# Other slots for the side jobs of a fused layer norm, attention and feed-forward kernel

## The chip, the cores and the metric

The kernel runs on one core of a Trainium2 chip. A core has TensorE (PE, the matrix engine), VectorE (DVE), ScalarE (ACT), GpSimd (POOL) and SyncE (SP), which here only issues DMAs. Each runs its own instruction list in order and waits on semaphores. The metric is the device time of one execution in microseconds (us), lower is better. Three runs of the kernel before gave 820.67, 822.58 and 823.44 us; the median is 822.58.

## The reference

For an input x of 16 batches, 512 tokens and 256 features:

```
xn  = layernorm(x)                              # no gain or offset
q, k, v = split(xn @ w_qkv.T + b_qkv)           # 16 heads of width 16
att = q @ k.T / 4 + bias[head, i - j]           # the bias hangs on the distance i - j
att = softmax(where(i >= j, att, -inf))         # causal
a   = (att @ v) @ w_proj.T + b_proj
f   = fp8(bf16(xn) / s_in) @ fp8(kernel / s_k) * s_in * s_k + ffn_bias
out = x + a + f
```

The position bias is folded into the score product as more rows of q and k, so one product of 64 rows a head gives scores and bias. Products in full precision are made of three products of a high and a low part.

## The kernel before

**Units and slots.** A batch is four units (g = 0 to 3) of four heads. A unit has 12 slots (k = 0 to 11). In each slot TensorE makes one block of transposed scores for the unit at hand (scores_T, line 611) into one of three PSUM banks scoreT_a to scoreT_c, and one block of plain scores two units ahead (scores, line 592) into one of three banks score_a to score_c. Slots 0 to 3 are blocks 512 wide, 4 to 7 are 384 wide, 8 to 11 are two tiles, 256 and 128 wide (of transposed scores; the plain ones likewise). In units 0 and 1 the transposed scores take a second product per tile, from the tile low_features (line 630).

**Who empties the banks.** ScalarE turns each transposed block into probs with an exponential (line 897). VectorE takes the row maximum of each plain block (line 975, two instructions a tile). The maxima of a unit are transposed by TensorE (job MT), negated and copied by ScalarE (max_T, line 819) and sent by SyncE (line 326) into the rows that the transposed scores of the next unit read. With three banks, slot n waits for the exponential of slot n - 3 (line 621) and for the maximum of slot n - 3 (line 600).

**Side jobs.** Between two slots TensorE does one side job, by a table of (unit, slot) pairs at the top of the file: PV (probabilities times v for the unit before, line 649, with the MT job inside it after its first tile), QK (four jobs a batch, each a q or k part of the next batch, line 537), V (two), FF (the fp8 product, two, line 580), PJ (output projection, two), T (two transposes of the normalised x of the batch after next, line 545). I call the slots between two jobs a spell. The jobs write the two banks misc_a and misc_b in turn, in the order in which they come (ORDER, MISC_BANK), and each waits until the job before it in its bank has been read out (misc, line 524).

**Read-outs.** ScalarE and VectorE read the job banks at places of the same kind of table, between exponentials and maxima: out_T (line 873) after PV, at slot OUT_AT; QK_evac (line 807, a copy of twice the width) and then QK_lo on VectorE (line 963); V_evac (line 792); FF (line 923); XH_evac and XB_evac (lines 796 and 799) and then T_lo on VectorE (line 957) for T. Since an engine's list is in order, an exponential that stands behind a read-out waits until that job is done. GpSimd masks the probs per third of a unit (line 1173) and does wide elementwise work between (lines 1161 to 1212).

**The loop.** Each engine's list is four bodies: batch 0, a loop over batches 1 to 13, batch 14, and batch 15.

Of the kernel before, what the change touches and what calls it, by code (L numbers as in the profile page):

```python
# [48 lines left out]

PV_AT = [(1, 3), (2, 3), (3, 3), (0, 3)]
MT_AT, FIRST_MT_AT = [(0, 3), (1, 3), (2, 3), (3, 3)], (0, 5)
QK_AT = [(0, 6), (0, 9), (1, 6), (1, 9)]
V_AT = [(2, 6), (2, 9)]
FF_AT = [(2, 0), (2, 0)]
PJ_AT = [(3, 0), (3, 6)]
T_AT, FIRST_T_AT = (3, 9), (0, 1)


OUT_AT = 4
FIRST_MT_OUT_AT = (0, 6)

MAX_AT, FIRST_MAX_AT = 2, (0, 4)
QK_HI_AT, QK_LO_AT = [(0, 6), (0, 9), (1, 6), (1, 9)], [(0, 7), (0, 10), (1, 7), (1, 10)]
V_OUT_AT = [(2, 6), (2, 9)]
AH_AT = [(2, 2), (2, 3)]
FF_OUT_AT = [(2, 0), (2, 1)]
RESULT_AT = [(3, 1), (3, 6)]
NORM_AT = [(3, 1), (3, 3), (3, 4), (3, 6)]  # L70
XH_AT, FIRST_XH_AT = [(3, 9), (3, 10)], [(0, 2), (0, 2)]
XL_AT, FIRST_XL_AT = [(3, 10), (0, 0)], [(0, 3), (0, 3)]

INVERT_AT, LAST_INVERT_AT = (0, 8), (3, 8)
STATS_AT, AGGR_AT = [(1, 2), (1, 3), (1, 5), (1, 8)], (1, 9)
MAGIC_AT = [(2, 0), (2, 1), (2, 2)]


EARLY = 4
# [6 lines left out]
ORDER = [(KINDS[kind], i) for _, kind, i in sorted((at, kind, i) for kind, ats in enumerate(  # L86
    (PV_AT, MT_AT, QK_AT, V_AT, FF_AT, PJ_AT, [T_AT, T_AT])) for i, at in enumerate(ats))]
assert len(ORDER) % 2 == 0
# [37 lines left out]
def build(nc, x, w_qkv, b_qkv, w_proj, b_proj, pos, ffn_w, s_in, s_k, ffn_b, feat_q, feat_k, out):  # L126
    with ExitStack() as ctx:
# [386 lines left out]
        def _(pe):  # L514
# [96 lines left out]
            def scores_T(b, g, k, first):  # L611


                n = SLOTS * g + k
                rows, u = rows_of(HU * g + k % 4)
                if k == 0:
                    if isinstance(b, int) and b == 0 and g < 2:
                        pe.wait_ge(feat_loaded[g], 64)
                    pe.wait_ge(max_loaded[g], 64 * (b + 1))
                if n >= 3 or not first:  # L620
                    pe.wait_ge(exp_done, ROW * b + n - 2)
                tiles = [k // 4] if k < 8 else [2, 3]
# [93 lines left out]
            def body(b, first, last, more):  # L716
# [62 lines left out]
        def _(act):  # L779
# [101 lines left out]
            def body(b, first, last, more):  # L881
                for g in range(G):
                    for k in range(SLOTS):
                        pb, pg = (b, g - 1) if g else (b - 1, 3)
                        if (g, k) == FIRST_MAX_AT if first and g == 0 else k == MAX_AT:
                            if not (last and g == 3):
                                max_hi(*((b, g + 1) if g < 3 else (b + 1, 0)))
                        if k == OUT_AT and not (first and g == 0):
                            if not (last and g == 3):
# [10 lines left out]
                        if not last:  # L900
# [38 lines left out]
        def _(dve):  # L939
# [133 lines left out]
            def body(b, first, last, more):  # L1073
                for g in range(G):
                    nb, ng = (b, g + 2) if g < 2 else (b + 1, g - 2)
                    ahead = not (last and g >= 2)
                    for k in range(SLOTS):
# [54 lines left out]
        def _(pool):  # L1132
# [55 lines left out]
            def add_bias(b):  # L1188
                pool.wait_ge(xn_ready, TT * (b + 1))
                pool.wait_ge(bp_made, 1)  # L1190
                xs = x_slot(b)
                GP.tensor_tensor(xs, xs, BP[:, :].unsqueeze(1).broadcast_to([P, TT, C]), ALU.add) \
                    .then_inc(xp_ready, 1)
# [83 lines left out]
            def body(b, first, last, more):  # L1277
                for g in range(G):
                    if g == 0:
                        quant_round(b)  # L1280
                    if g == 1 and not last:
                        quant_scale(b + 1)
                    if g == 2 and more:
                        rstd(b + 2)
                    if g == 3:
                        add_bias(b)
                    mask(b, g, 0)
                    if g == 0:
                        quant_write(b)
                        v_beside_ones(b, first)  # L1290
                    if g == 2 and not first:
                        attn_parts(b - 1)
                    if g == 3:
                        add_ffn(b)
                    mask(b, g, 1)
                    if g == 2:
                        ffn_bias(b)
                    if g == 1 and not first:
                        divide(b - 1)
                    mask(b, g, 2)  # L1300
# [35 lines left out]
```

## Time and profile before

| | |
|---|---|
| median of three runs | 822.58 us |
| the profiled execution | 822.72 us |
| its span | 821.0 us |
| busy share of the span | PE 92%, DVE 76%, ACT 71%, POOL 64% |
| TensorE clock in the steady part | full |
| one steady batch | 46.65 us (336.94 to 383.59) |

The span is what the profiler saw between first and last instruction; the execution is 1.7 us longer. The setup takes about the first 56 us, then 16 batches follow. In the timelines a row gives the start from the span's begin and the duration. Matmuls overlap, and their ends are modelled, so the time a job takes is read as the distance from its first start to the first start of what follows it.

### The profile page before, as it was taken

How to read it: one execution, taken by the hardware profiler on the slowest of the kernel's cores; microseconds unless marked ns; L12 is line 12 of the kernel's file. 1: busy time of each engine (PE TensorE's matmuls, PEld its weight loads, DVE VectorE, ACT ScalarE, POOL GpSimd, SP SyncE). 2: the span in 40 equal slices, each digit the busy share in tenths (PEclk: the TensorE clock that was granted, in tenths of full speed). 3: DMA queues.
4: the chain of work that ended last, by engine and by line, in shares of the span. 5: the costliest groups of instructions: out<-in, count | busy, mean ns of one | idle time of the engine just before them, and what ended most of it. 6: DMA issues, size and time to landing. Idle time of an engine off the chain costs nothing.

```text
span 821.0 us, 23167 instructions
## 1 busy us (share of the span) xinstructions
PE 756.7 (92%) x6313; PEld 521.4 (64%) x6313; DVE 627.6 (76%) x2395; ACT 585.5 (71%) x1258; POOL 529.1 (64%) x525
## 2 busy tenths in 40 slices
PE   6879999999999999999999999999999999999983
PEld 4556666676666767676666667666676667666552
DVE  3767878887878888887887888787887888787602
ACT  4246767777777868877786878877786787776650
POOL 6434568677676768677576867677676867757460
PEclk9759999999999999999999999999999999999885
DMA  5845666567765676667666666676567656766202
GB/s 170 158 77 100 113 154 115 138 132 140 152 134 139 122 163 116 135 148 142 133 134 151 117 149 124 133 159 136 134 134 157 116 135 137 144 132 130 65 17 84
DMA packets 55548, 106.07 MB, mean 129 GB/s; under 512 B 10464, under 2 KB 30432, under 8 KB 55520
## 3 DMA queue, kind: packets, MB, share of 16 engines
q1 hardware_dynamic: 55048, 105.19, 61.0%
q10 hardware_dynamic: 472, 0.54, 0.2%
q8 instruction: 13, 0.21, 0.1%
q14 instruction: 15, 0.12, 0.0%
HBM read 18.68 MB, written 8.91 MB: 34 GB/s over the span
## 4 chain that ended last, share of the span: by engine, by line
PE 58%; ACT 9%; SPq 8%; issue 8%; DVE 8%; DMA 6%; DVEq 1%; ACTq 1%; POOL 0%; POOLq 0%
PE misc_a L649 12%; PE misc_a L537 10%; SPq L326 7%; PE misc_b L537 7%; PE scoreT_b L627 6%; PE scoreT_a L627 5%; PE score_c L604 4%; PE misc_b L649 3%; PE score_a L604 3%; ACT probs L897 3%; ACT qk_parts L807 2%; DVE row_max L975 2%; DMA stacks<-neg_max_T 2%; ACT xnT_hi L796 2%; PE misc_b L588 2%
## 5 line engine op out<-in xcount | busy, mean ns | idle before, releaser
L1173 POOL TENSOR_SCALAR_AFFINE_SELECT probs<-probs 128x512 f32<-128x512 f32 x256 | 160.7, 640 | 243.4 <-ACT probs L897 241.6
L975 DVE CUSTOM_DVE_ANT_0 score_b<-score_b,causal_mask_q 128x384 f32<-128x384 f32 (+3 forms) x321 | 161.9, 521 | 122.1 <-PE score_b L604 121.8
L975 DVE CUSTOM_DVE_ANT_0 score_a<-score_a,causal_mask_q 128x512 f32<-128x512 f32 x319 | 173.2, 559 | 7.7 <-PE score_a L604 3.5
L975 DVE CUSTOM_DVE_ANT_0 score_c<-score_c,causal_mask_q 128x256 f32<-128x256 f32 (+3 forms) x384 | 171.4, 473 | 1.8 <-PE score_a L604 1.7
L897 ACT ACTIVATE probs<-scoreT_a 128x512 f32<-128x512 f32 (+1 forms) x256 | 145.0, 566 | 9.3 <-PE scoreT_a L630 6.4
L897 ACT ACTIVATE probs<-scoreT_b 128x384 f32<-128x384 f32 (+1 forms) x256 | 133.8, 523 | 24.4 <-PE scoreT_b L627 18.7
L975 DVE DVE_READ_ACCUMULATOR2_ANT row_max<- 128x1 f32 x1024 | 142.9, 140 | 0.0
L897 ACT ACTIVATE probs<-scoreT_c 128x384 f32<-128x384 f32 (+1 forms) x256 | 135.7, 530 | 8.2 <-PE scoreT_c L630 7.5
L649 PE MATMUL misc_a<-probs,v_ones 128*32 128x128 f32 (+3 forms) x1536 | 132.9, 442 | 0.4 <-POOL probs L1173 0.4
L627 PE MATMUL scoreT_a<-stacks 64*128 64x512 f32 (+3 forms) x320 | 109.5, 362 | 14.3 <-DMA low_features<-neg_max_T 7.5
L627 PE MATMUL scoreT_b<-stacks 64*128 64x384 f32 (+3 forms) x320 | 119.8, 394 | 2.3 <-ACT probs L897 2.0
L604 PE MATMUL score_b<-stacks 64*128 64x384 f32 (+3 forms) x321 | 118.8, 402 | 0.3 <-DVE row_max L975 0.2
L604 PE MATMUL score_a<-stacks 64*128 64x512 f32 x319 | 110.9, 379 | 3.2 <-DVE row_max L975 2.4
L627 PE MATMUL scoreT_c<-stacks 64*128 64x256 f32 (+3 forms) x384 | 105.4, 307 | 9.0 <-ACT probs L897 9.0
L604 PE MATMUL score_c<-stacks 64*128 64x256 f32 (+3 forms) x384 | 100.1, 314 | 7.2 <-DVE row_max L975 7.0
L627 PEld LDWEIGHTS scoreT_b<-stacks 64*128 64x128 f32 x320 | 57.0, 185 | 58.6 <-issue 27.8
L627 PEld LDWEIGHTS scoreT_c<-stacks 64*128 64x128 f32 x384 | 68.9, 187 | 16.0 <-ACT probs L897 14.1
L649 PEld LDWEIGHTS misc_a<-probs,v_ones 128*32 128x32 f32 x1536 | 59.9, 109 | 29.3 <-issue 12.9
L604 PEld LDWEIGHTS score_c<-stacks 64*128 64x128 f32 x384 | 66.8, 190 | 14.0 <-DVE row_max L975 13.9
L627 PEld LDWEIGHTS scoreT_a<-stacks 64*128 64x128 f32 x320 | 57.9, 188 | 24.8 <-issue 11.7
L604 PEld LDWEIGHTS score_a<-stacks 64*128 64x128 f32 x319 | 55.6, 189 | 17.9 <-DVE row_max L975 13.7
L873 ACT ACTIVATE out_T<-misc_a 128x512 f32<-128x512 f32 x48 | 28.7, 599 | 43.1 <-PE misc_a L649 42.7
(241 smaller groups left out, 1963.4 us busy)
## 6 DMA issues: line engine op xcount, KB each, us to landing
stacks<-qk_parts SPq DMA_DIRECT2D x128, 512.0 KB, 8.2
x_ring<-in_L_attn_x SPq DMA_DIRECT2D x16, 512.0 KB, 3.5
attn<-out_T SPq DMA_DIRECT2D x64, 128.0 KB, 2.6
xn<-recips SPq DMA_DIRECT2D x31, 256.0 KB
out<-x_ring SPq DMA_DIRECT2D x15, 512.0 KB, 3.0
stacks<-neg_max_T SPq DMA_DIRECT2D x128, 4.0 KB
low_features<-neg_max_T SPq DMA_DIRECT2D x124, 4.0 KB
low_features<-probs SPq DMA_DIRECT2D x8, 128.0 KB, 5.0
```

The source lines that it names most:

```text
L326: eng.dma_start(max_rows(g, h), MTS[2 * TT * h:2 * TT * h + 2 * TT, g % 2, :].bitcast(F32)) \
L537: last = mm(o, l(ct), r(ct), start=(ct == 0 and i == 0), stop=(ct == CT - 1 and i == 2))
L588: last = mm(bank[0:HU * 2 * TT, 0:P], MX[:, g % 2, 32 * part:32 * part + 32], ident[:, :], start=(part == 0), stop=(part == 1))
L604: last = mm(SB_[n % 3][:, o:o + w], STK[rows, u, 0, P * qt:P * qt + P], STK[rows, u, 1, 0:w], start=True, stop=True)
L627: last = mm(bank, STK[rows, u, 1, P * j:P * j + P], STK[rows, u, 0, P * j:T], start=True, stop=(g >= 2))
L649: last = mm(bank[32 * i:32 * i + 32, P * j:T], VA[:, j, HU * g + i, :, :].rearrange("p d a -> p (d a)"), probs(g, j)[:, i, :], start=(j == ...
L796: A(XH[:, ct, :], misc_of("T", ct)[:, :], ACT.Copy).then_inc(xh_ready, 1)
L807: A(qk_part(m, 0), misc_of("QK", m)[:, :].unsqueeze(1).broadcast_to([P, 2, T]), ACT.Identity, bias=BQ[:, bias:bias + 1]).then_inc(qh_ready, 1)
L873: A(OT[:, :], misc_of("PV", g)[:, :], ACT.Copy).then_inc(ot_ready, 1)
L897: A(probs_slot(g, k), STB[(SLOTS * g + k) % 3][:, 0:w], ACT.Exp).then_inc(exp_done, 1)
L975: last = V.tensor_tensor_reduce(bank, bank, CMQ[:, T - w:T], 1.0, LEAST, ALU.add, ALU.max, MX[:, g % 2, 8 * h + 4 + qt:8 * h + 5 + qt])
L1173: last = GP.affine_select(out=d, in_=d, compare_op=ALU.is_ge, fill=0.0, base=0, pattern=[[0, HU], [1, P]], channel_multiplier=-1)
```

## The change

The table of places is another one, and two GpSimd operations change places. The tables say (unit, slot):

```diff
-PV_AT = [(1, 3), (2, 3), (3, 3), (0, 3)]
+PV_AT = [(1, 2), (2, 2), (3, 2), (0, 2)]
-QK_AT = [(0, 6), (0, 9), (1, 6), (1, 9)]
-V_AT = [(2, 6), (2, 9)]
-FF_AT = [(2, 0), (2, 0)]
-PJ_AT = [(3, 0), (3, 6)]
-T_AT, FIRST_T_AT = (3, 9), (0, 1)
-OUT_AT = 4
+QK_AT = [(0, 6), (0, 10), (1, 6), (1, 10)]
+V_AT = [(2, 5), (2, 8)]
+FF_AT = [(2, 11), (2, 11)]
+PJ_AT = [(3, 5), (3, 8)]
+T_AT, FIRST_T_AT = (3, 10), (0, 1)
+OUT_AT = 3
...
@@ gpsimd body
                     if g == 3:
-                        add_bias(b)
+                        ffn_bias(b)
                     mask(b, g, 0)
...
                     if g == 2:
-                        ffn_bias(b)
+                        add_bias(b)
```

A job comes after its slot. The read-outs move with their jobs: QK_evac to (0, 6), (0, 10), (1, 6), (1, 10) and QK_lo one slot later; V_evac to (2, 5) and (2, 8); the FF read-outs to (2, 11) and (3, 0); the result sums to (3, 5) and (3, 8); XH_evac and XB_evac to (3, 10) and (3, 11); T_lo to (3, 11) and (0, 0). The inversion of the denominators moves from (0, 8) to (0, 7), the statistics of x from slots 2, 3, 5 and 8 of unit 1 to 2, 2, 3 and 3, their aggregation from slot 9 to 5, the three fp8 steps of VectorE from slots 0, 1 and 2 of unit 2 to 2, 2 and 3, and one normalisation from (3, 6) to (3, 7).

So the spells before are slots 4 to 6, 7 to 9 and 10 to 3 in unit 0, and now 3 to 6, 7 to 10, and 11 to 2. No amount of work changes.

First place: ScalarE in unit 1 of batch 0 (the loop has the same order), from the read-out of PV to the second read-out of QK. Before:

```order
L819 ACTIVATE neg_max_T<-misc_b 32x128
L873 ACTIVATE out_T<-misc_a 128x512
L897 ACTIVATE probs<-scoreT_b 128x384
L897 ACTIVATE probs<-scoreT_c 128x384
L897 ACTIVATE probs<-scoreT_a 128x384
L807 ACTIVATE qk_parts<-misc_a,b_qkv 128x2x512
L897 ACTIVATE probs<-scoreT_b 128x384
L897 ACTIVATE probs<-scoreT_c 128x384
L897 ACTIVATE probs<-scoreT_a 128x384
L807 ACTIVATE qk_parts<-misc_b,b_qkv 128x2x512
```

and now:

```order
L819 ACTIVATE neg_max_T<-misc_b 32x128
L873 ACTIVATE out_T<-misc_a 128x512
L897 ACTIVATE probs<-scoreT_a 128x512
L897 ACTIVATE probs<-scoreT_b 128x384
L897 ACTIVATE probs<-scoreT_c 128x384
L897 ACTIVATE probs<-scoreT_a 128x384
L807 ACTIVATE qk_parts<-misc_a,b_qkv 128x2x512
L897 ACTIVATE probs<-scoreT_b 128x384
L897 ACTIVATE probs<-scoreT_c 128x384
L897 ACTIVATE probs<-scoreT_a 128x384
L897 ACTIVATE probs<-scoreT_b 128x384
L807 ACTIVATE qk_parts<-misc_b,b_qkv 128x2x512
```

The read-out of PV (out_T) stood ahead of slot 4's exponential and now stands ahead of slot 3's; between two read-outs there are now four exponentials, not three.

Second place: TensorE in unit 3 of batch 0, around the T job (line 545). Before:

```order
L627 MATMUL scoreT_a<-stacks 128x256
L604 MATMUL score_a<-stacks 128x256
L627 MATMUL scoreT_a<-stacks 128x128
L604 MATMUL score_a<-stacks 128x128
L545 MATMUL misc_a<-ident_f,xn 128x128 x4
L545 MATMUL misc_b<-ident_f,xn 128x128 x4
L627 MATMUL scoreT_b<-stacks 128x256
L604 MATMUL score_b<-stacks 128x256
L627 MATMUL scoreT_b<-stacks 128x128
L604 MATMUL score_b<-stacks 128x128
L627 MATMUL scoreT_c<-stacks 128x256
L604 MATMUL score_c<-stacks 128x256
```

and now:

```order
L627 MATMUL scoreT_b<-stacks 128x256
L604 MATMUL score_b<-stacks 128x256
L627 MATMUL scoreT_b<-stacks 128x128
L604 MATMUL score_b<-stacks 128x128
L545 MATMUL misc_a<-ident_f,xn 128x128 x4
L545 MATMUL misc_b<-ident_f,xn 128x128 x4
L627 MATMUL scoreT_c<-stacks 128x256
L604 MATMUL score_c<-stacks 128x256
L627 MATMUL scoreT_c<-stacks 128x128
L604 MATMUL score_c<-stacks 128x128
```

The two transposes come one slot later, ahead of slot 11 alone.

Third place: VectorE in the loop, from the end of one batch to the start of the next; xnT_lo are the two T_lo, L975 the row maxima. Before:

```order
L957 TENSOR_TENSOR xnT_lo<-misc_a,xnT_hi 128x512
L332 REGISTER_ALU
L975 ISA score_c,row_max<-score_c,causal_mask_q 128x256
L975 ISA row_max 128x1
L975 ISA score_c,row_max<-score_c,causal_mask_q 128x128
L975 ISA row_max 128x1
L1108 REGISTER_ALU
L1108 COMPARE_AND_BRANCH
L975 ISA score_a,row_max<-score_a,causal_mask_q 128x512
L975 ISA row_max 128x1
L957 TENSOR_TENSOR xnT_lo<-misc_b,xnT_hi 128x512
```

and now:

```order
L975 ISA score_c,row_max<-score_c,causal_mask_q 128x256
L975 ISA row_max 128x1
L975 ISA score_c,row_max<-score_c,causal_mask_q 128x128
L975 ISA row_max 128x1
L956 ISA
L957 TENSOR_TENSOR xnT_lo<-misc_a,xnT_hi 128x512
L1108 REGISTER_ALU
L1108 COMPARE_AND_BRANCH
L975 ISA score_a,row_max<-score_a,causal_mask_q 128x512
L975 ISA row_max 128x1
L957 TENSOR_TENSOR xnT_lo<-misc_b,xnT_hi 128x512
```

T_lo of the first half stood ahead of slot 11's maxima and now stands behind them; that of the second half stays behind slot 0's.

## Rows read from the trace of the kernel before

**Rows 1.** Windows, one middle batch and the last: length, busy and count per engine, PEclk, DMA.

```profile
336.94:383.59 46.65, 44.68 (x396) 31.23 (x400) 38.47 (x149) 36.22 (x79) 32.46 (x32) 1.00 0.66 138
756.40:821.00 64.60, 45.68 (x347) 29.30 (x344) 20.89 (x75) 28.22 (x62) 26.08 (x24) 0.74 0.21 60
```

**Rows 2.** Timeline, TensorE, a middle batch's first unit: start, duration, line, operation.

```profile
383.52 1.06 PE L649 MATMUL misc_a<-probs,v_ones 128*32 128x512 f32 x8
...
386.23 0.44 PE L627 MATMUL scoreT_b<-stacks 64*128 64x384 f32 x1
...
386.51 0.33 PE L630 MATMUL scoreT_b<-low_features 64*128 64x384 f32 x1
...
387.03 0.34 PE L630 MATMUL scoreT_a<-low_features 64*128 64x384 f32 x1
...
387.30 0.50 PE L537 MATMUL misc_a<-xnT_hi,w_qkvT_hi 128*128 128x512 f32 x1
...
388.90 0.44 PE L627 MATMUL scoreT_b<-stacks 64*128 64x384 f32 x1
...
390.08 0.50 PE L537 MATMUL misc_b<-xnT_hi,w_qkvT_hi 128*128 128x512 f32 x1
...
391.68 0.38 PE L627 MATMUL scoreT_b<-stacks 64*128 64x256 f32 x1
...
394.66 0.50 PE L604 MATMUL score_c<-stacks 64*128 64x512 f32 x1 [0.45 <-DVE row_max L975]
...
395.74 1.07 PE L649 MATMUL misc_a<-probs,v_ones 128*32 128x512 f32 x8
```

**Rows 3.** Timeline, ScalarE, the same unit.

```profile
386.53 0.60 ACT L873 ACTIVATE out_T<-misc_a 128x512 f32<-128x512 f32 x1 [1.22 <-PE misc_a L649]
...
387.03 0.48 ACT L897 ACTIVATE probs<-scoreT_b 128x384 f32<-128x384 f32 x1
...
389.14 1.12 ACT L807 ACTIVATE qk_parts<-misc_a,b_qkv 128x1024 fp32r<-128x1024 f32 x1 [0.86 <-PE misc_a L537]
...
390.16 0.48 ACT L897 ACTIVATE probs<-scoreT_b 128x384 f32<-128x384 f32 x1
...
395.88 0.60 ACT L897 ACTIVATE probs<-scoreT_a 128x512 f32<-128x512 f32 x1
```

**Rows 4.** Timeline, TensorE, the other three units of that batch.

```profile
405.37 0.50 PE L627 MATMUL scoreT_a<-stacks 64*128 64x512 f32 x1 [0.56 <-DMA stacks<-neg_max_T]
...
405.99 0.61 PE L580 MATMUL misc_a<-ffn_w_q,xq 128*128 128x256 bf16 x4
...
406.96 0.50 PE L627 MATMUL scoreT_b<-stacks 64*128 64x512 f32 x1
...
407.93 1.06 PE L649 MATMUL misc_a<-probs,v_ones 128*32 128x512 f32 x8
...
416.63 0.39 PE L537 MATMUL misc_a<-w_projT_hi,attn_hi 128*128 128x256 f32 x1
...
418.26 0.49 PE L627 MATMUL scoreT_b<-stacks 64*128 64x512 f32 x1
...
419.15 1.07 PE L649 MATMUL misc_b<-probs,v_ones 128*32 128x512 f32 x8
...
425.42 0.66 PE L545 MATMUL misc_a<-ident_f,xn 128*128 128x128 f32 x4
...
426.44 0.38 PE L627 MATMUL scoreT_b<-stacks 64*128 64x256 f32 x1
...
430.30 1.06 PE L649 MATMUL misc_a<-probs,v_ones 128*32 128x512 f32 x8
```

**Rows 5.** Timeline, ScalarE, end of the batch's fourth unit.

```profile
426.24 0.62 ACT L796 ACTIVATE xnT_hi<-misc_a 128x512 fp32r<-128x512 f32 x1
...
427.19 0.54 ACT L897 ACTIVATE probs<-scoreT_b 128x384 f32<-128x384 f32 x1
```

**Rows 6.** Timeline, VectorE, start of the next batch.

```profile
429.66 0.68 DVE L957 TENSOR_TENSOR xnT_lo<-misc_b,xnT_hi 128x512 fp32r<-128x512 f32 x1
```

More of the change, by code:

```diff
@@ L47 @@
 QUERY_TILES = [(3,)] * 4 + [(2,)] * 4 + [(1, 0)] * 4
-PV_AT = [(1, 3), (2, 3), (3, 3), (0, 3)]
-MT_AT, FIRST_MT_AT = [(0, 3), (1, 3), (2, 3), (3, 3)], (0, 5)
-QK_AT = [(0, 6), (0, 9), (1, 6), (1, 9)]
-V_AT = [(2, 6), (2, 9)]
-FF_AT = [(2, 0), (2, 0)]
-PJ_AT = [(3, 0), (3, 6)]
-T_AT, FIRST_T_AT = (3, 9), (0, 1)
-OUT_AT = 4
+PV_AT = [(1, 2), (2, 2), (3, 2), (0, 2)]
+MT_AT, FIRST_MT_AT = [(0, 2), (1, 2), (2, 2), (3, 2)], (0, 5)
+QK_AT = [(0, 6), (0, 10), (1, 6), (1, 10)]
[4 more added lines that the diff above has]
+OUT_AT = 3
 FIRST_MT_OUT_AT = (0, 6)
 MAX_AT, FIRST_MAX_AT = 2, (0, 4)
-QK_HI_AT, QK_LO_AT = [(0, 6), (0, 9), (1, 6), (1, 9)], [(0, 7), (0, 10), (1, 7), (1, 10)]
-V_OUT_AT = [(2, 6), (2, 9)]
+QK_HI_AT, QK_LO_AT = [(0, 6), (0, 10), (1, 6), (1, 10)], [(0, 7), (0, 11), (1, 7), (1, 11)]
+V_OUT_AT = [(2, 5), (2, 8)]
 AH_AT = [(2, 2), (2, 3)]
[L68 to L76, printed above, removed]
+FF_OUT_AT = [(2, 11), (3, 0)]
+RESULT_AT = [(3, 5), (3, 8)]
+NORM_AT = [(3, 1), (3, 3), (3, 4), (3, 7)]
+XH_AT, FIRST_XH_AT = [(3, 10), (3, 11)], [(0, 2), (0, 2)]
+XL_AT, FIRST_XL_AT = [(3, 11), (0, 0)], [(0, 3), (0, 3)]
+INVERT_AT, LAST_INVERT_AT = (0, 7), (3, 8)
+STATS_AT, AGGR_AT = [(1, 2), (1, 2), (1, 3), (1, 3)], (1, 5)
+MAGIC_AT = [(2, 2), (2, 2), (2, 3)]
 EARLY = 4
```

## The prediction

> **What bounds the kernel now.** I read the windows first. In a steady batch of 46.65 us TensorE is busy 44.68, VectorE 38.47, ScalarE 36.22 and GpSimd 32.46 us, with TensorE's clock at 1.00, its upper level of 2.4 GHz [rows 1]. TensorE sets the time, but its busy figure hides short waits, so I went on to its timeline and measured each job and spell from first start to next start. I count a unit from its PV job to the next PV job.
>
> Unit 0 of a batch before [rows 2]: PV 2.71 (383.52 to 386.23), three slots 1.07, QK 1.60 (387.30 to 388.90), three slots 1.18, QK 1.60, six slots 4.06 (391.68 to 395.74), in all 12.22. The spells of three slots have no wait, since three banks take three slots. The spell of six has: the fourth block of its kind waited 0.45 for VectorE's maximum at 394.66. Unit 1 is 12.19 long with the FF job in it (395.74 to 407.93), unit 2 11.22 and unit 3 11.15 (to 430.30) [rows 2, 4]; the four are 46.78.
>
> The rule for what follows: the fourth slot of a spell can't start before the exponential of the spell's first slot is done. That exponential stands behind the read-out of the job just ended. So the price of a read-out at a spell's head is paid by TensorE as soon as the spell has four slots.
>
> **ScalarE's answer after a job** [rows 3]. After PV: out_T starts 3.01 after PV's start (386.53), the exponential behind it 0.50 later. After a QK job: the copy starts 1.84 after the job's start (389.14 after 387.30), the exponential 1.02 later (390.16) and takes 0.48, so it ends 3.34 after the job's start. A 512 wide exponential takes 0.60 (395.88). I add 0.05 for the semaphore, an estimate: in the row of 387.30 the job starts right behind the last product, so the gap is small, and ends of 0 and 0.1 move the sum by under 0.3 a batch.
>
> **What a slot costs when it had to wait.** Its two first products start together, the third 0.28 later (386.23, 386.51), and the job follows 0.27 after the last one (387.03, 387.30) [rows 2]: 0.55 for a 384 wide slot, and I take 0.58 for the two tiles of slot 10 (four starts instead of two, shorter each). A 512 wide slot with low_features I put at 0.65, by width from the same rows, and one without at 0.43, from 0.89 for three of them (418.26 to 419.15) [rows 4] plus what a restart loses (0.28 against 0.17 between 386.23, 386.51 and its followers).
>
> **Unit 0 after.** Slots 3 to 6: slot 3's exponential starts at 3.01 + 0.50 = 3.51, ends at 4.11, slot 6 starts at 4.16 and QK at 4.71. Without the wait TensorE would have been there at 2.71 + 1.07 + about 0.48 for slot 3 = 4.26. Slots 7 to 10: slot 10 starts 3.39 after QK's start, the next QK 3.97 after it. TensorE would have been ready at 1.60 + 1.18 = 2.78, so it stands 0.6. Slots 11 to 2: slot 2 again 3.39 after QK's start, PV 4.04 after it. VectorE isn't the later one here, by an estimate: slot 11's scores are there about 2.2 after QK's start, its maxima take under 0.8, so they end near 3.0, ahead of 3.39. Sum 4.71 + 3.97 + 4.04 = 12.72, against 12.22.
>
> **Unit 1 after.** The same with slots of unit 2 at the end, which have no low_features: 4.71 + 3.97 + 3.39 + 0.43 = 12.50. Before it was 12.19 with FF (0.97, 405.99 to 406.96) in it [rows 4]; without FF 11.22. The wait of 0.56 for the negated maxima at 405.37 [rows 4] goes: from PV to that slot are now 4.71 + 3.97 + 1.60 + 0.29 = 10.57 against 9.63, and that chain starts from PV. Nothing is won by it, since slot 2 of that spell waits for ScalarE anyway.
>
> **Unit 2 after** has spells of three only: PV 2.71, slots 0.95, V 1.63, slots 0.80, V 1.63, slots 0.83, FF 0.97, slots 0.95 (V as PJ0, 416.63 to 418.26; slots from the 0.89 above, less for narrower ones, with 0.1 for a job that waits for out_T's read-out, which ends 3.61 after PV's start when TensorE comes at 3.58). Sum 10.47.
>
> **Unit 3 after.** PV 2.71, slots 0.95, PJ 1.63, slots 0.80, PJ 1.63, slots 9 and 10 0.62, T 1.02 (425.42 to 426.44) [rows 4]: T begins at 8.34 and ends at 9.36. Then slots 11, 0, 1 to about 10.35. The copies of the first transpose can start 0.82 after T (426.24), at 9.16, and the two take 0.95 (to 427.19) [rows 5]; slot 11's exponential runs from 10.11 to 10.6; slot 2 starts at 10.65, PV at 11.30, against 11.15. Before, both pairs of copies stood ahead of slot 11's exponential; now only one does, but T also comes a slot nearer to PV. The gain of the one goes into the other.
>
> **One new wait.** The MT job sits in PV, 0.88 after its start, and needs the bank of the second transpose, which T_lo of the second half reads last. That is 0.68 long [rows 6] and stands behind slot 0's maxima and behind the second pair of copies, which end about 11.65. T_lo ends near 12.45; MT is due at 12.18. 0.3 a batch, ends 0 and 0.7 (all of a T_lo late). Before, one slot more lay between them and the job had come a slot earlier.
>
> **GpSimd's swap** I cost at nothing: GpSimd is busy 32.46 of 46.65 [rows 1], both operations are one pass over the same 1024 columns, and PV reads the last third's masks only in its second half. What hides them is that half PV; if the cover went, the late part would add to PV one for one.
>
> **The sum.** 12.72 + 12.50 + 10.47 + 11.30 + 0.30 = 47.29, against 46.65 to 46.78. The even units 2 and 3 (FF counted on both sides, 23.34 before) win 1.3; units 0 and 1 (23.44 before) lose 1.8. That is +0.5 to +0.6 a batch. 14 batches (1 to 14) have this form: +8. Batch 0 lacks PJ and its unit 0 is fixed elsewhere: about -0.4; the last batch has no QK, V or T, and I take 0. So 822.7 + 8 = 831 in the profiled execution, which lies 0.1 from the median of the runs: 831. Its own range is 826 to 836, from 0.2 to 0.95 a batch.
>
> **A rule against the clock.** In the steady window above the clock stands at 1.00 although TensorE waits several times a batch, and in the last batch, busy 45.68 of 64.60, at 0.74 [rows 1]. After the change I have it busy about 44.7 of 47.3, near the first row, so the sum has the clock unchanged. The Trainium skill, "TensorE: Matmul & The Clock Gate", section "A second HAM failure mode: psum-queue depth-cycling", says that a kernel that goes through its PSUM banks with a short pause between groups can make the clock swing between its two levels. By that rule six more pauses a batch could bring it down; this trace doesn't bear it out so far.
>
> **The rivals.**
> - *Faster, the even spells pay.* For: units 2 and 3 get rid of 1.3 us, and the spell of six is gone, which took 4.06 where six slots at 1.18 / 3 are 2.36. The point from which it decides is the fourth slot's wait in units 0 and 1: there are six such slots a batch, so if each costs 0.10 less than I worked out, the change is worth nothing, and with 0.2 less (a restart that overlaps with the job behind it) a batch takes 46.1: 822.7 - 14 x 0.6 = 814. Against: the order of ScalarE's list leaves the exponential no way past the copy. Chance 0.23.
> - *No change*, the same with 0.10 less each: 820.1 to 825. Chance 0.15.
> - *More than forecast.* T_lo and MT cost 0.7, a block of QK's copies is late as well, and TensorE's spells restart slower: +1 us a batch more, 845. The chain of negated maxima could also be late in unit 2: the stack copies ahead of it on SP now wait for the QK_lo of a job that comes a slot later. By the sum above that QK_lo ends 0.37 before PV, so it has to be over a microsecond late to matter. Chance 0.10.
> - *The forecast*, 825 to 836: 0.52.
>
> **How the numbers follow.** About 0.3% (2.5 us) is what a measurement can tell from no change. Slower holds the forecast and the third rival, 0.62; same 0.15; faster 0.23. The range of 8 in 10 is 816 to 840: below it lies half of the faster case (0.12 to 0.14), above it half of the third rival.
>
> **What would show it.** In the profile after: the QK jobs of units 0 and 1 start 4.7 and 8.7 after PV; ahead of slots 6, 10 and 2 there TensorE waits for ScalarE's exponential, not for VectorE; VectorE has more idle time ahead of its maxima there; units 2 and 3 have no wait in three-slot spells and take 10.5 and 11.3; in PV of unit 0 MT waits for VectorE's T_lo; the wait for the negated maxima in unit 2 is gone. I am wrong if a batch takes under 46.7, or if units 0 and 1 together are under 24.5.

## The result, and the profile after

The changed kernel takes 845.42 us (median of four runs, 844.79 to 846.42) against 823.00 us in the runs beside it: a ratio of 1.0279, 95% interval 1.0256 to 1.0303. It is slower, as forecast, but by 22 us where 8 were forecast, and outside the range of 816 to 840. It is also the time that the third rival had named (845), but not by that rival's terms, as shown below.

The unit ledger answers to [rows 2, 4]. First the windows of the changed kernel: one steady batch, then its units 0, 2 and 3. The columns are those of [rows 1].

```profile
343.83:392.33 48.50, 45.33 (x392) 31.22 (x393) 38.93 (x149) 36.22 (x80) 32.48 (x32) 1.00 0.64 133
343.83:356.86 13.03, 11.84 (x96) 7.66 (x97) 10.08 (x37) 9.17 (x20) 8.04 (x7) 1.00 0.61 118
369.17:380.06 10.89, 10.79 (x103) 7.98 (x101) 9.72 (x36) 8.89 (x22) 9.58 (x11) 1.00 0.70 120
380.06:392.33 12.27, 11.53 (x104) 8.12 (x104) 9.00 (x36) 10.02 (x24) 6.97 (x8) 1.00 0.58 130
```

The batch has grown from 46.65 to 48.50, with the clock still at 1.00 and ScalarE's busy time where it was (36.22 in both). In us, from PV start to PV start, with FF and PJ where each kernel has them:

| unit | before | forecast | after |
|---|---|---|---|
| 0 | 12.22 | 12.72 + 0.30 | 13.03 |
| 1 | 12.19 | 12.50 | 12.31 |
| 2 | 11.22 (most batches 11.1) | 10.47 | 10.89 |
| 3 | 11.15 | 11.30 | 12.27 |
| sum | 46.78 (46.66 in most) | 47.29 | 48.50 |

TensorE's timeline in the changed kernel, unit 0, is as forecast but for its second row:

```profile
343.83 1.06 PE L649 MATMUL misc_a<-probs,v_ones 128*32 128x512 f32 x8
...
345.12 0.40 PE L588 MATMUL misc_b<-ident_f,row_max 128*32 128x128 f32 x2 [0.23 <-ACT row_max L815]
...
346.97 0.49 PE L627 MATMUL scoreT_a<-stacks 64*128 64x512 f32 x1
...
348.41 0.44 PE L627 MATMUL scoreT_a<-stacks 64*128 64x384 f32 x1 [0.19 <-ACT probs L897]
...
348.96 0.50 PE L537 MATMUL misc_a<-xnT_hi,w_qkvT_hi 128*128 128x512 f32 x1
...
352.35 0.38 PE L627 MATMUL scoreT_b<-stacks 64*128 64x256 f32 x1 [0.54 <-ACT probs L897]
...
352.95 0.50 PE L537 MATMUL misc_b<-xnT_hi,w_qkvT_hi 128*128 128x512 f32 x1
...
356.20 0.50 PE L627 MATMUL scoreT_c<-stacks 64*128 64x512 f32 x1 [0.24 <-ACT probs L897]
...
356.86 1.07 PE L649 MATMUL misc_a<-probs,v_ones 128*32 128x512 f32 x8
```

Slots 6, 10 and 2 wait for ScalarE; from QK to QK it is 3.99 (forecast 3.97). In the row of 345.12 is what was not forecast: MT inside PV waits for `row_max L815`, ScalarE's max_hi. In unit 3 this is the whole story. TensorE, then ScalarE, changed kernel:

```profile
379.35 0.39 PE L627 MATMUL scoreT_c<-stacks 64*128 64x512 f32 x1
...
379.63 0.50 PE L604 MATMUL score_c<-stacks 64*128 64x512 f32 x1
...
380.06 1.06 PE L649 MATMUL misc_a<-probs,v_ones 128*32 128x512 f32 x8
...
381.70 0.40 PE L588 MATMUL misc_b<-ident_f,row_max 128*32 128x128 f32 x2 [0.57 <-ACT row_max L815]
...
383.54 0.49 PE L627 MATMUL scoreT_a<-stacks 64*128 64x512 f32 x1
```

```profile
379.80 0.68 ACT L923 ACTIVATE xnT_bf<-misc_b,ffn_scales 128x512 bf16<-128x512 f32 x1
380.37 0.60 ACT L897 ACTIVATE probs<-scoreT_b 128x512 f32<-128x512 f32 x1
380.85 0.61 ACT L826 ACTIVATE xn<-x_ring,neg_mean_rstd,rstd 128x256 f32 x1
381.34 0.23 ACT L815 ACTIVATE row_max<-row_max 128x32 fp32r<-128x32 f32 x1
381.45 0.60 ACT L897 ACTIVATE probs<-scoreT_c 128x512 f32<-128x512 f32 x1
```

Two rows of the kernel before, MT in unit 0 (PV at 383.52) and in unit 3 (PV at 419.15):

```profile
384.40 0.38 PE L588 MATMUL misc_b<-ident_f,row_max 128*32 128x128 f32 x2
...
420.38 0.38 PE L588 MATMUL misc_a<-ident_f,row_max 128*32 128x128 f32 x2 [0.16 <-DVE x_ring L988]
```

In the changed kernel PV starts at 380.06 and MT is due at 380.94 (0.88 later, as at 383.52 and 384.40 before). But max_hi, the copy of the maxima that MT reads (line 815), takes 0.23 and ends at 381.57, since ScalarE's list has it ahead of slot 2's exponential, behind slot 1's, a normalisation and the FF read-out, which the change put there. PV takes 3.48 where the forecast had 2.71. Before it took 3.05, since MT waited for the first result sum in its bank; that wait is gone, and a longer one has come. The table's MAX_AT stayed at 2 when PV went from 3 to 2, so the copy lost the slot of lead that it had had.

The waits of TensorE over the steady part (105 to 755 us), changed kernel; columns: total us, times, longest:

```profile
PE scoreT_b L627 <- ACT probs L897: 13.0, 28, 0.5
PE misc_b L588 <- ACT row_max L815: 10.5, 26, 0.6
PE scoreT_c L627 <- ACT probs L897: 7.9, 22, 0.5
PE scoreT_a L627 <- ACT probs L897: 6.3, 28, 0.4
```

Before, the same stretch had 8.1 us of waits for ScalarE's exponentials (slot 2 behind T in unit 3), 6.2 for VectorE's maxima (the kind of [rows 2] at 394.66) and 6.1 for DMAs of maxima (the kind of [rows 4] at 405.37). The last two kinds are gone. 27.2 of exponentials and 10.5 of max_hi stand for them.

### The profile page after: what moved, and what is told of

Its sections match the earlier page's. It is cut to its first block, busy times and chain, and to the rows that moved or that the text cites. A ratio compares the mean times of both kernels' runs of the same rounds, so it can differ in the third digit from the quotient of the medians.

```text
span 843.1 us, 23154 instructions
## 1 busy us (share of the span) xinstructions
PE 762.0 (90%) x6313; PEld 521.5 (62%) x6313; DVE 634.7 (75%) x2395; ACT 586.1 (70%) x1258; POOL 529.8 (63%) x525
## 4 chain that ended last, share of the span: by engine, by line
PE 61%; ACT 19%; issue 11%; DMA 4%; ACTq 2%; DVE 1%; SPq 1%; POOL 0%; POOLq 0%; DVEq 0%
PE misc_a L649 15%; PE misc_a L537 12%; PE misc_b L537 12%; ACT probs L897 10%; PE scoreT_a L627 5%; PE scoreT_c L627 3%; PE misc_b L588 3%; PE scoreT_b L627 3%; ACT qk_parts L807 2%; ACT out_T L873 2%; PE score_b L604 2%; PE score_c L604 1%; ACT xnT_bf L923 1%; ACT xnT_bf L799 1%; ACT xnT_hi L796 1%
## 5 line engine op out<-in xcount | busy, mean ns | idle before, releaser
L975 DVE CUSTOM_DVE_ANT_0 score_a<-score_a,causal_mask_q 128x512 f32<-128x512 f32 x319 | 170.2, 550 | 102.3 <-PE score_a L604 98.1
L975 DVE CUSTOM_DVE_ANT_0 score_b<-score_b,causal_mask_q 128x384 f32<-128x384 f32 (+3 forms) x321 | 166.2, 534 | 26.3 <-PE score_b L604 26.3
L975 DVE CUSTOM_DVE_ANT_0 score_c<-score_c,causal_mask_q 128x256 f32<-128x256 f32 (+3 forms) x384 | 173.1, 478 | 15.7 <-PE score_c L604 12.0
L649 PE MATMUL misc_a<-probs,v_ones 128*32 128x512 f32 (+3 forms) x2048 | 176.4, 442 | 2.3 <-POOL probs L1173 0.8
L975 DVE DVE_READ_ACCUMULATOR2_ANT row_max<- 128x1 f32 x1024 | 144.0, 141 | 0.0
L627 PE MATMUL scoreT_a<-stacks 64*128 64x512 f32 (+3 forms) x320 | 121.8, 401 | 11.5 <-ACT probs L897 7.9
L604 PE MATMUL score_a<-stacks 64*128 64x512 f32 x319 | 118.0, 401 | 3.5 <-DVE row_max L975 2.9
L627 PE MATMUL scoreT_c<-stacks 64*128 64x256 f32 (+3 forms) x384 | 111.7, 324 | 9.9 <-ACT probs L897 9.5
L627 PE MATMUL scoreT_b<-stacks 64*128 64x384 f32 (+3 forms) x320 | 103.8, 344 | 14.0 <-ACT probs L897 14.0
L604 PE MATMUL score_c<-stacks 64*128 64x256 f32 (+3 forms) x384 | 107.3, 333 | 4.9 <-DVE row_max L975 4.6
L649 PEld LDWEIGHTS misc_a<-probs,v_ones 128*32 128x32 f32 x2048 | 79.6, 110 | 44.2 <-issue 22.3
L604 PE MATMUL score_b<-stacks 64*128 64x384 f32 (+3 forms) x321 | 101.0, 347 | 0.3 <-DVE row_max L975 0.2
L873 ACT ACTIVATE out_T<-misc_a 128x512 f32<-128x512 f32 x64 | 38.3, 599 | 78.0 <-PE misc_a L649 78.0
L807 ACT ACTIVATE qk_parts<-misc_a,b_qkv 128x1024 fp32r<-128x1024 f32 x32 | 35.8, 1117 | 39.1 <-PE misc_a L537 39.1
```

The lines of the kernel that those rows point to most:

```text
L604: last = mm(SB_[n % 3][:, o:o + w], STK[rows, u, 0, P * qt:P * qt + P], STK[rows, u, 1, 0:w], start=True, stop=True)
L649: last = mm(bank[32 * i:32 * i + 32, P * j:T], VA[:, j, HU * g + i, :, :].rearrange("p d a -> p (d a)"), probs(g, j)[:, i, :], start=(j == ...
L807: A(qk_part(m, 0), misc_of("QK", m)[:, :].unsqueeze(1).broadcast_to([P, 2, T]), ACT.Identity, bias=BQ[:, bias:bias + 1]).then_inc(qh_ready, 1)
L873: A(OT[:, :], misc_of("PV", g)[:, :], ACT.Copy).then_inc(ot_ready, 1)
L975: last = V.tensor_tensor_reduce(bank, bank, CMQ[:, T - w:T], 1.0, LEAST, ALU.add, ALU.max, MX[:, g % 2, 8 * h + 4 + qt:8 * h + 5 + qt])
```

## The experiments

Times are medians. The kernel before was measured anew beside each group: 821.3 us beside e1 to e4, 821.9 beside e6 to e9, 821.8 beside e10 to e13. The ratios and their 95% intervals are to those runs, as measured, and differ from the quotients of the medians by up to 0.2%. Diffs show only the table's main lines: MT_AT moves with PV_AT, and QK's read-outs with QK_AT.

**The missing slot of lead.** Two kernels: the changed one with max_hi a slot earlier, and the kernel before with max_hi a slot later.

```diff
# e1_max_early, on the changed kernel
-MAX_AT, FIRST_MAX_AT = 2, (0, 4)
+MAX_AT, FIRST_MAX_AT = 1, (0, 4)
# e2_before_max_late, on the kernel before
-MAX_AT, FIRST_MAX_AT = 2, (0, 4)
+MAX_AT, FIRST_MAX_AT = 3, (0, 4)
```

> The changed kernel with one number turned back in spirit: max_hi, the copy on ScalarE that MT reads, stands ahead of slot 1's exponential, not ahead of slot 2's (MAX_AT 1 for 2). Theory A (MT inside PV waits for that copy, which now has slot 0's and 1's exponentials and the read-outs ahead of it): unit 3 falls from 12.27 to about 11.5, unit 0 from 13.03 to 12.7 or 12.8, the others stay; some 1.0 us a batch, 845.4 - 14 = 831. Theory B (the whole of the loss is in the fourth slots' waits for exponentials): nothing moves, 844 to 846. Theory C (T_lo holds MT's bank, as the prediction had it): unit 0 keeps its 3.14 for PV and only unit 3 changes.

> The kernel before with max_hi one slot later (MAX_AT 3 for 2), so that copy and PV stand to each other as in the changed kernel. Theory A: MT waits here too, in unit 3 and at the start of unit 0, where ScalarE is latest; 0.3 to 0.9 us a batch, 827 to 835. Theory B: 821 to 825.

e1: 832.50 us, ratio 1.0130 (1.0080 to 1.0180), 13 us under the changed kernel. e2: 832.32, ratio 1.0128 (1.0079 to 1.0176), 11 over the kernel before. Theory A (MT waits for max_hi) holds from both sides. In e1, PV of unit 3 and of unit 0:

```profile
373.52 1.07 PE L649 MATMUL misc_a<-probs,v_ones 128*32 128x512 f32 x8
374.40 0.38 PE L588 MATMUL misc_b<-ident_f,row_max 128*32 128x128 f32 x2
...
376.23 0.49 PE L627 MATMUL scoreT_a<-stacks 64*128 64x512 f32 x1
...
385.02 1.06 PE L649 MATMUL misc_a<-probs,v_ones 128*32 128x512 f32 x8
386.15 0.41 PE L588 MATMUL misc_b<-ident_f,row_max 128*32 128x128 f32 x2
```

Unit 3's MT starts 0.88 after PV and PV takes 2.71. Unit 0's starts 1.13 after, so PV is 2.98: these 0.27 are the wait for T_lo that the prediction had at 0.30 (the second T_lo ends at 386.10; one row of the waits names `DVE xnT_lo L957`). In e2 the wait appears in a kernel that never had it, mostly in PV of unit 2, behind FF, which takes 3.63, and by 0.17 in unit 3; the expectation had named units 3 and 0:

```profile
364.66 1.06 PE L649 MATMUL misc_a<-probs,v_ones 128*32 128x512 f32 x8
...
366.45 0.40 PE L588 MATMUL misc_b<-ident_f,row_max 128*32 128x128 f32 x2 [0.72 <-ACT row_max L815]
```

A control, the kernel before with max_hi a slot earlier than it needs (MAX_AT 1):

> The kernel before with max_hi one slot earlier (MAX_AT 1 for 2). A control: before, MT doesn't wait for that copy, so theory A gives no change, 820 to 824. A gain of more than 0.5% would say that the copy's place matters by something else than MT's wait.

822.60 us, ratio 0.9994 (0.9968 to 1.0020): no change. The copy's place matters only where MT waits for it.

**The copy ahead of the exponential.** The changed kernel with QK's copy behind the exponential of the spell's first slot:

```diff
# e3_copy_behind, on the changed kernel
-QK_HI_AT, QK_LO_AT = [(0, 6), (0, 10), (1, 6), (1, 10)], [(0, 7), (0, 11), (1, 7), (1, 11)]
+QK_HI_AT, QK_LO_AT = [(0, 7), (0, 11), (1, 7), (1, 11)], [(0, 8), (0, 12), (1, 8), (1, 12)]
```

> The changed kernel with QK's copy on ScalarE one place later, behind the exponential of the spell's first slot (slots 7 and 11), and QK_lo on VectorE one place later too. Theory B (the exponential that stands behind the copy is what slots 10 and 2 wait for): these four waits a batch go, QK to QK falls from 3.99 to about 3.2 and QK to PV from 3.91 to about 3.3, 2.2 to 2.8 us a batch, 845.4 - 35 = 810 (805 to 820). Rival D (VectorE is next in line: its QK_lo now delays the maxima of slots 8 and 0): half of that, 825 to 835. If the waits for exponentials don't cost anything by themselves: 843 to 847.

843.88 us, ratio 1.0266 (1.0219 to 1.0312): nearly nothing, and the forecast of 810 is missed. But the spell that it was about did change. From QK (349.83) to QK (353.22) it is 3.39, not 3.99, so slot 10's wait is gone whole. ScalarE:

```profile
352.08 0.49 ACT L897 ACTIVATE probs<-scoreT_b 128x384 f32<-128x384 f32 x1 [1.65 <-PE scoreT_b L630]
352.47 1.11 ACT L807 ACTIVATE qk_parts<-misc_a,b_qkv 128x1024 fp32r<-128x1024 f32 x1
```

So the mechanism is right for slot 10 and its yield went elsewhere, to a new wait of MT, now in PV of unit 2 also. There max_hi stands behind QK's last copy and two exponentials, and that copy starts 0.83 ahead of PV (368.30), where it started 1.98 ahead of it in the changed kernel:

```profile
369.13 1.06 PE L649 MATMUL misc_a<-probs,v_ones 128*32 128x512 f32 x8
370.63 0.40 PE L588 MATMUL misc_b<-ident_f,row_max 128*32 128x128 f32 x2 [0.44 <-ACT row_max L815]
```

and to the last spell of unit 0, 2.62 for 2.32, where some batches now wait for the DMAs of the maxima. With both edits (e6), and with out_T behind slot 3's exponential as well in units 0 and 1 (e7, `OUT_AT = [4, 4, 3, 3]`, which takes max_T, the copy of the negated maxima, along):

> The changed kernel with both edits: max_hi one slot earlier and QK's copy behind one exponential. Alone, the first gave 832.5 and the second 843.9, where the second took 0.6 from QK to QK but left PV of unit 2 at 3.35, waiting for max_hi. If the gain of the second was only hidden by MT's wait, the two together give more than their sum: PV of units 2 and 3 back to 2.71, 0.64 + 0.79 + 0.2 off e3's 48.25 a batch, 822 (818 to 826). If the second edit's gain was lost elsewhere (row maxima, copies of stacks), 829 to 832.

> As e6_both, and out_T in units 0 and 1 one place later, behind slot 3's exponential. Slot 6's wait is for that exponential; it goes: PV to QK falls by 0.4 to 0.5 in both units, 0.9 a batch, 12 us under e6. Rival: QK in misc_a waits for out_T itself, which now ends about 4.1 after PV's start where QK comes at 4.26: under 2 us of loss.

e6: 827.39, ratio 1.0064 (1.0040 to 1.0088). e7: 826.01, ratio 1.0050 (1.0035 to 1.0065). The second edit is worth 1.5 us alone and 5 with the first in place: part was hidden by MT's wait. e6 stays 5 above the 822 expected. In most batches PV of unit 2 takes 2.96 to 3.02 there, not 2.71, some 4 us in all, since MT now waits for its bank: QK_lo of the last QK job reads it last, and it moved a place with the copy. It ends at 361.59 (e6, VectorE, then TensorE, PV at 360.48):

```profile
360.85 0.74 DVE L963 SCALAR_TENSOR_TENSOR qk_parts<-misc_b,b_qkv,qk_parts 128x512 fp32r<-128x512 f32 x1
```

```profile
361.65 0.41 PE L588 MATMUL misc_b<-ident_f,row_max 128*32 128x128 f32 x2
```

e7 yields 1.4 where 12 were expected, and that isn't clear of the noise. In its profile QK still starts 4.75 (unit 1) and 5.13 (unit 0) after PV, where e6 has 4.79 and 4.97. Slot 6 starts 4.13 and 4.41 after PV, in e6 4.25 and 4.42. So the read-out had cost slot 6 only 0.12 and 0.01. What is left is slot 3's own way through ScalarE: its scores, then an exponential of 0.60. QK then waits for out_T in misc_a, as the rival said, though out_T ends 4.7 after PV's start and not 4.1. Unit 1 of e7, PV at 394.78, ScalarE, then TensorE:

```profile
398.26 0.60 ACT L897 ACTIVATE probs<-scoreT_a 128x512 f32<-128x512 f32 x1 [2.51 <-PE scoreT_a L630]
...
398.91 0.57 ACT L873 ACTIVATE out_T<-misc_a 128x512 f32<-128x512 f32 x1
```

```profile
398.91 0.44 PE L627 MATMUL scoreT_a<-stacks 64*128 64x384 f32 x1 [0.16 <-ACT probs L897]
...
399.53 0.51 PE L537 MATMUL misc_a<-xnT_hi,w_qkvT_hi 128*128 128x512 f32 x1
```

**Fewer slots a spell.** Three kernels move jobs back, e4 (PV and out_T) in all four units, e8 and e9 in units 0 and 1:

```diff
# e4_pv_back, on the changed kernel: PV and out_T
-PV_AT = [(1, 2), (2, 2), (3, 2), (0, 2)]
+PV_AT = [(1, 3), (2, 3), (3, 3), (0, 3)]
-OUT_AT = 3
+OUT_AT = 4
# e8_qk_three, on e1_max_early: QK and its read-outs behind slots 5 and 8
-QK_AT = [(0, 6), (0, 10), (1, 6), (1, 10)]
+QK_AT = [(0, 5), (0, 8), (1, 5), (1, 8)]
# e9_hybrid, on the changed kernel: units 0 and 1 of before, 2 and 3 as changed
-PV_AT = [(1, 2), (2, 2), (3, 2), (0, 2)]
-QK_AT = [(0, 6), (0, 10), (1, 6), (1, 10)]
-OUT_AT = 3
-MAX_AT, FIRST_MAX_AT = 2, (0, 4)
+PV_AT = [(1, 3), (2, 2), (3, 2), (0, 3)]
+QK_AT = [(0, 6), (0, 9), (1, 6), (1, 9)]
+OUT_AT = [4, 4, 3, 3]
+MAX_AT, FIRST_MAX_AT = [2, 2, 1, 1], (0, 4)
```

> The changed kernel with PV, MT and their read-outs back behind slot 3 (PV_AT, MT_AT, OUT_AT of before), all else as changed. Spells in units 0 and 1 are then slots 4 to 6, 7 to 10, 11 to 3. Theory A: MT's wait in PV goes by this too, since max_hi is again a slot ahead. Theory B: slot 6's wait goes, slot 10's stays at 3.99 from QK to QK, and the last spell has slot 3 to pay. Together 1.0 (A) and about 0.3 (B) a batch less: 828 to 834. If only A holds: 831; if neither, 843 to 847.

> As e1_max_early (832.5), with QK behind slots 5 and 8 instead of 6 and 10, so units 0 and 1 have spells 3 to 5, 6 to 8 and 9 to 2. If a spell's fourth slot is what costs, four of the six waits go and one long spell is left: unit 0 about 12.4, unit 1 about 11.5, 1.2 a batch less, 815. If the number of slots in a spell doesn't matter, 830 to 835.

> Units 0 and 1 with the slots of before (PV 3, QK 6 and 9), units 2 and 3 as changed, max_hi at slot 2 and 1. If the ledger by unit holds when the halves are put together: unit 0 12.22, unit 1 11.4, unit 2 10.9, unit 3 11.8, together 46.3 against 46.66 before: 817, faster than before by 0.5%. If the halves lean on each other, 822 to 830.

e4: 853.60, ratio 1.0367 (1.0319 to 1.0414). e8: 837.20, ratio 1.0193 (1.0166 to 1.0219). e9: 829.98, ratio 1.0088 (1.0061 to 1.0115). All three miss, to the slow side, for more than one reason. From the timelines, in unit 0 (spells between jobs, us; e8's over all batches):

| kernel | spells of unit 0 | unit 0 | unit 3 |
|---|---|---|---|
| before | 1.07, 1.18, 4.06 | 12.22 | 11.15 |
| changed | 1.99, 2.39, 2.32 | 13.03 | 12.27 |
| e1 | 1.98, 2.39, 2.32 | 12.86 | 11.50 |
| e8 | 1.18, 1.13, 3.99 to 4.52 | 12.2 to 13.0 | 11.5 |
| e9 | 1.07, 1.18, 4.10 | 12.27 | 12.77 |
| e4 | 1.07, 2.40, 3.16 | 12.53 | 12.65 |

The reason that all three share: taking slots out of the first spells puts them into the last, where they cost 0.8 to 1.1 each in units 0 and 1 and 1.3 in unit 3, about what they had cost at their old places (0.80 and 1.26 from e1 to e8 in unit 0) or more. There TensorE waits for ScalarE, for VectorE (8.0 us of waits for maxima in e9) and for the DMAs of the maxima (9.4 us in e8, 5.9 in e9).

In e4 MT's wait did go (PV 2.71 in units 0 to 2), and yet the kernel is slower than the changed one: slot 3 came behind a copy into a spell of five (3.16), and behind the copies of the transposes (3.32 in unit 3). In units 2 and 3 taking slot 3 out of the first spell brings nothing, since V and PJ now come two slots behind PV and wait 0.33 and 0.28 for out_T, 0.6 a batch. Over the steady part:

```profile
PE misc_a L537 <- ACT out_T L873: 7.9, 26, 0.3
```

In e8 and e9 the clock comes in. The rows are windows of PV of unit 2 of e9 in two batches, a part of the second, and the start of a PV of unit 1 in e11, which follows; the last columns are PEclk, DMA share and GB/s:

```profile
364.61:367.32 2.71, 2.71 (x38) 1.58 (x38) 2.68 (x8) 1.54 (x4) 2.40 (x5) 1.00 0.95 145
411.84:416.24 4.40, 4.40 (x38) 2.16 (x37) 2.71 (x8) 1.54 (x4) 2.50 (x5) 0.61 0.95 164
412.50:413.44 0.94, 0.94 (x8) 0.18 (x1) 0.94 (x5) 0.62 (x2) 0.94 (x2) 0.50 0.82 83
368.13:369.00 0.87, 0.87 (x8) 0.21 (x9) 0.87 (x4) 0.60 (x1) 0.87 (x2) 0.50 0.49 186
```

In 5 of 14 batches of e9 and in 5 of e8 the granted clock falls to 0.50, the lower of its two levels (1.2 GHz), around PV of unit 2, which then takes 4.0 to 4.4. That is 8.4 us of the profiled execution of e9 (835.36) and 7.4 of e8's. The other three executions of e9 take 828 to 830 at a mean granted clock of 0.962 to 0.964, where the profiled one has 0.954, so e9's median of 829.98 hardly holds it. All four of e8 have 0.950 to 0.956, where e1's have 0.962 to 0.968. So e8's 837.20 holds it, and by my estimate (837.2 less 7.4) e8 would be near 830 at the full clock, a little under e1's 832.5.

At the full clock the hybrid keeps 12.27 and 11.29 in units 0 and 1 and 10.9 in unit 2, and loses it in unit 3, whose last spell of five behind T takes 3.33. The ledger by unit does hold for units 0 to 2; I had the slot that unit 3 gets back at 0.3, and it costs 1.3.

**The DMA of the maxima.** On e7, SyncE sends unit 1's maxima ahead of regrouping out_T:

```diff
                 load_stack(b, 3)
+                load_max(b, 1)
                 if not first:
                     regroup(b - 1, 3, False)
-                load_max(b, 1)
```

> As e7_out_behind (826.0), where unit 0's last spell (2.51 to 2.82) waits for the negated maxima that SyncE sends into low_features. SyncE sends them there ahead of out_T's regrouping instead of behind it, so about 1.5 us earlier. If the issue order is what makes them late: 0.3 to 0.5 a batch, 820 to 822. If they queue behind the 1 MB of stack copies in the DMA rings anyway, 825 to 827.

869.28 us, ratio 1.0578 (1.0519 to 1.0636). Neither answer: what stood behind the maxima is late now. The maxima go out 4.5 us after unit 0's PV, in e7 7.0, but SyncE waits for them in its list (165.9 us over the steady part for `neg_max_T`, 93.3 in e7), and the denominators go out 8.3 after PV, in e7 5.8. VectorE's inversion waits for the denominators, and with it the maxima of the spell; VectorE, then TensorE:

```profile
363.49 0.55 DVE L982 RECIPROCAL denominators_inv<-denominators 128x64 f32<-128x64 f32 x1 [2.65 <-DMA denominators<-out_T]
```

```profile
364.73 0.38 PE L604 MATMUL score_c<-stacks 64*128 64x256 f32 x1 [1.33 <-DVE row_max L975]
...
365.98 0.50 PE L604 MATMUL score_a<-stacks 64*128 64x512 f32 x1 [0.53 <-DVE row_max L975]
```

Unit 0's last spell takes 4.84 on average for 2.65 in e7, 31 of the 43 us. The other 12 are in PV of unit 1, 3.65 on average for 2.71, where the clock falls behind this stop (368.13 above). So whether the issue order makes the maxima late in e7 stays open.

**The rule put to use on the kernel before.** The rule is that a read-out ahead of an exponential is paid by the fourth slot behind it. Two edits: the second pair of copies of the transposes behind slot 11's exponential, then also the first result sum of VectorE a place earlier, since MT in unit 3 waits for it.

```diff
# e10_t_apart, on the kernel before
-XH_AT, FIRST_XH_AT = [(3, 9), (3, 10)], [(0, 2), (0, 2)]
-XL_AT, FIRST_XL_AT = [(3, 10), (0, 0)], [(0, 3), (0, 3)]
+XH_AT, FIRST_XH_AT = [(3, 9), (3, 11)], [(0, 2), (0, 2)]
+XL_AT, FIRST_XL_AT = [(3, 10), (0, 1)], [(0, 3), (0, 3)]
# e12_t_result: the same, and
-RESULT_AT = [(3, 1), (3, 6)]
+RESULT_AT = [(3, 0), (3, 6)]
```

> The kernel before, where in unit 3 both pairs of copies of the transposes (XH_evac, XB_evac, 0.95 us a pair) stand ahead of slot 11's exponential, for which slot 2 waits. Here the second pair stands behind it, and the second T_lo one place later. If the rule found (a read-out ahead of an exponential is paid by the fourth slot behind it) is what stretches that spell, it falls from 3.86 to about 3.4: 816 (813 to 820). Rival: VectorE's maxima are next in line and give back most of it, 820 to 823; or MT in misc_b now waits for T_lo and PV grows, 822 to 826.

> As e10_t_apart, and the first result sum on VectorE one place earlier, behind slot 0's maxima, where VectorE is idle. MT in unit 3 waits for it (PV 3.05 instead of 2.71). PV of unit 3 back to 2.71: 0.34 a batch, 5 us under e10. If MT then waits for something else, no difference to e10.

e10: 823.39, ratio 1.0000 (0.9973 to 1.0026). The rival holds. Slot 2 (scoreT_c, 382.93) no longer waits for ScalarE, but its plain half does for VectorE, and the spell is 3.86 as before:

```profile
382.93 0.39 PE L627 MATMUL scoreT_c<-stacks 64*128 64x512 f32 x1
...
383.79 0.49 PE L604 MATMUL score_c<-stacks 64*128 64x512 f32 x1 [0.47 <-DVE row_max L975]
```

e12: 816.90, ratio 0.9936 (0.9910 to 0.9963): faster than the kernel before by 0.6%, and than the changed one by 28 us. PV of unit 3 starts at 373.71, MT 0.89 later, and takes 2.74 instead of 3.05, which is 4.3 us over 14 batches of the 4.9 gained:

```profile
373.71 1.06 PE L649 MATMUL misc_b<-probs,v_ones 128*32 128x512 f32 x8
374.60 0.41 PE L588 MATMUL misc_a<-ident_f,row_max 128*32 128x128 f32 x2
```

Whether the second edit needs the first was not tried apart.

## Why the prediction was wrong

**The step that failed is "One new wait".** It looked at MT's bank and not at MT's operand. The wait for max_hi is nowhere in the sum, so it stood at nothing, and no reason is given. The table was at hand: MAX_AT is 2 in both kernels, so max_hi stands ahead of slot 2's exponential, while PV, with MT in it, follows slot 3 before and slot 2 now. Measured: 0.77 in unit 3 and 0.16 of the 0.43 in unit 0, 0.93 a batch; over 14 batches 13 us, and e1 gives back 12.9. e1's 832.50 is where the forecast of 831 had been, though in part by offsets. The rival *More than forecast* had 845 with T_lo and MT at 0.7, a late block of QK's copies and slower restarts. T_lo cost 0.27 and the restarts came as worked out (0.55, 0.60 and 0.66 in unit 0 for 0.55, 0.58 and 0.65), so that the measured time is its number is luck.

**The direction was right, its mechanism in part.** Slots 6, 10 and 2 of units 0 and 1 wait for the exponential of the spell's first slot. Forecast 4.71, 3.97 and 4.04 (unit 0), measured in e1, less the wait of MT, 4.69 (2.71 + 1.98), 3.98 (1.59 + 2.39) and 3.91. For slot 10 e3 shows that the read-out ahead of that exponential is what it pays for: with the copy behind, 3.99 becomes 3.39. For slot 6 e7 shows that it isn't: moving out_T takes 0.01 and 0.12 off. There the fourth slot pays for the way of the first slot's block through ScalarE. For slot 2 no run takes it apart: e3's last spell shrinks from 2.09 to 1.92 in unit 1 and grows in unit 0. T_lo's 0.30 is 0.27.

**Units 2 and 3 were put too low.** Unit 2 takes 10.89 for 10.47: its last spell is 1.29, not 0.95, as slot 2's plain scores start 0.28 late (379.35 and 379.63 above), behind the maximum of slot 11. Unit 3 without MT's wait is 11.50 for 11.30, with 0.98 for slots 6 to 8. Units 0 (with T_lo) and 1 were 0.17 and 0.19 too high. Together these make 0.26 a batch, and with MT's 0.93 the 1.2 between 47.29 and 48.50. The recorded gain of 1.3 in the even units is 1.57 by its own terms (23.34 less 21.77); with T_lo's 0.30 the sum is as it stands.

**The ends.** PV of batch 1's unit 0 comes 1.6 us earlier in the span (101.38 for 102.97), part of it because PV stands a slot earlier; I had 0.4 for batch 0. It offsets part of the above: 13 steady batches at 1.85 are 24 us, less 1.6 is 22.4, and the spans differ by 22.1.

**The points named ahead.** Units 0 and 1 together take 25.34, over the 24.5 named. VectorE is idle for 5.1 us there, where it was idle for 4.4. The wait for DMAs of maxima went, as said. "Units 2 and 3 have no wait in three-slot spells" was wrong at slot 2. The faster rival asked for 0.10 less in each of the six fourth slots; they came out within 0.15 of what was worked out, together 0.33 lower (in e1), a little over half of what that rival needed for no change. In the changed kernel the clock stayed at 1.00 in every steady unit, so the rule on pauses between groups changed nothing in its time. But in e8, e9 and e11 the clock did fall. Whether pauses are the reason stays open: e9's spell ahead of that PV has the same two waits (0.46 and 0.18) in a batch in which the clock holds, and e4, with 40 us of waits in the steady part, keeps 1.00.

**A habit that misled.** Of the twelve kernels, e3, e4, e6, e7, e8, e9, e10 and e11 came out slower than expected. Most took away a wait and priced its going in full, while the next one stood close behind: max_hi in e3 (0.44 in the row above), QK_lo in e6, out_T in e4 and e7, VectorE's maximum in e10 (0.47).

## What to carry to other kernels

When a job moves in a list that is kept by hand, go through everything the job reads as well as the bank it writes, and find where each producer stands in its own engine's list: a copy of 0.23 us one place too late cost 13 us. With three banks between two engines, the fourth block of a run waits for the first one's way through the reader, and for a read-out that stands ahead of it (0.6 us behind a copy of 1.1, at most 0.12 behind out_T), while a run of three doesn't. Evening out the distances turned the spells of three in units 0 and 1, which had no wait, into spells of four that wait. But slots taken out of one spell go into another, and e8 shows that this can cost as much. Take the price of a wait removed as an upper bound until the next releaser is known, and check both halves of a block that has two readers. Look at the granted clock of each stretch before a longer job is put down to a wait.

## What the runs showed of the hardware

A matmul pair that starts after a wait or a job change takes its third product 0.28 us after it (386.23 and 386.51 in [rows 2]), where in a row the next ones follow 0.17 to 0.18 apart (386.51, 386.69 and 386.86 in the same trace). So by this trace a stop costs TensorE about 0.1 us beside the wait itself, an estimate. The slots behind 348.41 and 352.35 above take 0.55 and 0.60 to the next job. The trace puts this time under busy: TensorE's busy time grew from 44.68 to 45.33 us a batch with the same products. So a busy share can rise with stops, and the distance from start to start is the better measure.

The granted clock can fall to its lower level (0.50) in the middle of a steady kernel and come back within a PV. PV of unit 2 then takes 4.40 us instead of 2.71 (e9, 411.84 and 364.61). Ahead of it TensorE had waited 0.46 and 0.18 in e9, 0.43 for a DMA in e8 (411.24) and 1.33 in e11 (364.73). Similar waits in other batches and kernels left it at 1.00, so what brings it down isn't shown.
